# Expert loop of a mixture-of-experts kernel: gathers first, scatters two rounds behind them

## What is computed

```
scores = softmax(xf @ gate_w.T)                     # 2048 tokens, 64 experts
topk_w, topk_idx = top_k(scores, 6)
buf_tok, buf_w = per expert, its tokens and weights (capacity 128)
gx = xp[buf_tok]                                    # gather: [64, 128, 512]
g, u = split(gx @ gate_up_proj, 2)                  # per expert, 512 -> 2 x 192
eo = (silu(g) * u) @ down_proj * buf_w[..., None]   # per expert, 192 -> 512
routed = zeros.at[buf_tok].add(eo)                  # scatter-add
shared = (silu(xf @ sh_gate.T) * (xf @ sh_up.T)) @ sh_down.T
out = x + routed + shared
```

## Time and profile before

| | |
|---|---|
| median of 3 runs | 702.58 us (699.43 to 702.7) |
| the profiled execution | 701.51 us |
| its span, first to last instruction | 699.7 us |
| TensorE's mean granted clock | 0.92 |
| TensorE busy | 84% |
| GpSimd busy | 49% |
| GpSimd's queue: 27248 packets, 43.55 MB | 32.4% of the DMA engines' span |
| SyncE's queue: 48240 packets, 93.22 MB | 43.7% |

### The profile page before, as it was taken

How to read it: one execution, slowest core, us unless ns; L and a number is a source line. 1 busy time by engine, 2 the same in 40 slices (tenths; PEclk the granted TensorE clock), 3 DMA queues, 4 the chain that set the end, 5 groups by cost and what they waited for, 6 DMA issues and landing times. The chain is left out here.

```text
span 699.7 us, 6458 instructions
## 1 busy us (share of the span) xinstructions
PE 584.8 (84%) x2035; PEld 314.2 (45%) x2035; DVE 229.2 (33%) x575; ACT 172.9 (25%) x352; POOL 346.3 (49%) x299
## 2 busy tenths in 40 slices
PE   5998928776889999999998799997969999873950
PEld 2444414544534555555554455553535545441520
DVE  3865632865742322222222122221212222220220
ACT  4666742475101111112111111210101111110100
POOL 1134755262140656565642756556256565653662
PEclk9999959878989999999999899998989999897895
DMA  8945334569332989999889799988989999898752
GB/s 229 250 130 92 51 84 155 207 201 292 109 109 81 264 236 251 278 240 276 252 241 259 157 274 257 274 249 182 225 205 267 233 275 243 249 285 174 158 61 35
DMA packets 78170, 141.46 MB, mean 202 GB/s; under 512 B 14576, under 2 KB 33520, under 8 KB 78128
## 3 DMA queue, kind: packets, MB, share of 16 engines
q1 hardware_dynamic: 48240, 93.22, 43.7%
q0 software_dynamic: 27248, 43.55, 32.4%
q10 hardware_dynamic: 2640, 4.20, 1.7%
HBM read 107.89 MB, written 33.04 MB: 201 GB/s over the span
## 5 line engine op out<-in xcount | busy, mean ns | idle before, releaser
L507 POOL DMA_INDIRECT out<-y,half_at x128 | 200.6, 1567 | 191.6 <-DMA out<-y,half_at 59.2
L785 PE MATMUL bank<-gu_w,gxT 128*128 128x384 f32 x512 | 177.4, 490 | 0.8 <-ACT gxT L957 0.8
L773 PE MATMUL bank<-dn_w,hidT 96*128 96x512 f32 x256 | 125.4, 613 | 0.9 <-DVE hidT L1232 0.9
L1215 DVE TENSOR_SCALAR y<-bank,gx 128x512 f32<-128x512 f32 x64 | 48.0, 751 | 225.5 <-PE bank L773 202.4
L785 PEld LDWEIGHTS bank<-gu_w,gxT 128*128 128x128 f32 x512 | 93.2, 192 | 52.6 <-issue 2.5
L664 PE MATMUL bank<-xnT,upT 128*128 128x512 f32 x192 | 94.1, 636 | 0.0
L965 ACT ACTIVATE eg<-bank 128x192 f32<-128x192 f32 x64 | 21.1, 330 | 288.8 <-PE bank L785 288.8
L514 POOL DMA_INDIRECT gx<-rows_dram,table x64 | 64.3, 1005 | 21.7 <-issue 17.1
L1227 DVE TENSOR_TENSOR hid<-bank,eg 128x192 f32<-128x192 f32 x64 | 31.7, 496 | 130.7 <-ACT eg L965 130.7
L765 PE MATMUL bank<-ident,gx 128*128 128x128 f32 x256 | 41.3, 287 | 36.0 <-DMA gx<-rows_dram,table 35.8
L773 PEld LDWEIGHTS bank<-dn_w,hidT 96*128 96x128 f32 x256 | 47.5, 197 | 48.3 <-issue 46.8
(11 more groups left out here) (167 smaller groups left out, 465.1 us busy)
## 6 DMA issues: line engine op xcount, KB each, us to landing
gu_w<-in_gate_up SPq DMA_DIRECT2D x128, 384.0 KB, 4.6
dn_w<-in_down SPq DMA_DIRECT2D x128, 192.0 KB, 5.8
x<-in_x SPq DMA_DIRECT2D x4, 1024.0 KB, 9.0
feat_dram<-feat SPq DMA_DIRECT2D x16, 256.0 KB, 3.8
rows_dram<-rows ACTq DMA_DIRECT2D x4, 1024.0 KB, 4.8
out<-x SPq DMA_DIRECT2D x4, 1024.0 KB, 5.7
out<-x POOLq DMA_DIRECT2D x3, 1024.0 KB, 11.7
out<-y,half_at POOLq DMA_INDIRECT x128, 5.4
```

The lines of the kernel that those rows point to most:

```text
L507: pool.indirect_dma_start(halves, bass.IndirectOffsetOnAxis(ap=half_at[:, h, e:e + 1], axis=0), y[:, e % YB, h * (D // 2):(h + 1) * (D // ...
L773: last = nc.tensor.matmul(DN[:], hidT[:, e % 2, j, :], dn_w[:, e % U, j, :], start=(j == 0), stop=(j == 1))
L785: last = nc.tensor.matmul(GU[e % 2][:, 0:2 * I], gxT[:, e % 2, c, :], gu_w[:, e % U, c, :], start=(c == 0), stop=(c == KC - 1))
L1215: nc.vector.tensor_scalar(y[:, e % YB, :], DN[:], gx[:, e % GX, D + e:D + e + 1], None, ALU.mult).then_inc(y_ready, 1)
```

## The change

The loop runs over two more rounds. Each round asks first for the gather of expert e+6, then scatters both halves of expert e-2 and, where it is due, issues the shared add, which stands behind the same scatters as before. Nothing else is changed: buffers, waits and the programs of the other engines are the same.

```diff
+LAG = 2
...
-                for e in range(E):
-                    scatter(e, 0)
-                    scatter(e, 1)
+                for e in range(E + LAG):
                     if e + GX < E:
                         gather(e + GX)
-                    if e + 1 < E and shared_before(e + 1) > shared_before(e):
+                    if e < LAG:
+                        continue
+                    d = e - LAG
+                    scatter(d, 0)
+                    scatter(d, 1)
+                    if d + 1 < E and shared_before(d + 1) > shared_before(d):
                         for h in range(2):
-                            pool.wait_ge(half_added[h], 16 * (e + 1))
-                        add_shared(shared_before(e + 1))
+                            pool.wait_ge(half_added[h], 16 * (d + 1))
+                        add_shared(shared_before(d + 1))
```

## The result

The changed kernel takes 715.05 us, median of four runs (711.3 to 717.51); the kernel before took 701.93 us in its four (699.43 to 702.7). The ratio is 1.017, 95% interval 1.012 to 1.022: **slower by 13 us**. The forecast was 712.0 us. A second trace of the same kernel, taken with the experiments, has a span of 713.7 us and is set beside it where the two differ.

What follows compares the result with a forecast made beforehand. The prediction took the chain of half scatters, each waiting for the landing before, as the bound. Its terms, 14.0 + 3.9 - 2.2 - 5.2 = +10.5 us on 701.5, gave 712.0 us, range 699 to 721.

Steps and rivals of the forecast that it cites:

- chain of scatters: Half h of expert e starts only when half h of expert e-1 has landed; sets the end from expert 9 on.
- Start of the chain: At the loop's start, scatter 0 waits behind gather 8, which needs y(2): 240.5 instead of 226.5, +14.0 us.
- 369 to 373: Sign in the profile after: the time in us at which scatter 19 would start.
- low end of 10.6: If landings were quicker, y(21) would still hold scatter 19 to 369.1, so the late start costs at least +10.6 us.
- First shared add: Behind the first add, weights keep streaming, so rounds 22 and 23 lose their 5.05 us pace: +3.9 us, low end nothing.
- Second and third add: TensorE starved as before; half the difference between rounds of 23.8 and 19.4 us gained: -2.2 us, between 0 and -4.4.
- Tail: Last rounds: nine scatter rounds without gathers instead of six, four of them at 4.6 us: -5.2 us, or nothing.
- TensorE's waits: TensorE would wait for gathers less, 15 to 30 us, and none at the first add over 2 us.
- Rival A: Loop bound by feeding TensorE and the DMA engines; loaded scatter rounds fall to 6.6 us: -11, 690 us; chance 0.15.
- One sign that the forecast had named for A: Scatter rounds between the adds taking under 6.7 us would show the forecast wrong.
- Rivals B and C: B: no change, +1, 702.5 us, chance 0.11. C: weights stream through every add, +21, 723 us, chance 0.06.

Runs made afterwards that it cites:

- late lag: The kernel before up to scatter 19 and the first shared add, the order of the change from there on (gather e+8 ahead of scatter e): 698.2 us, ratio 1.000.
- no lag: The change with LAG 0 instead of 2, gather e+6 still ahead of scatter e: 711.6 us, ratio 1.019; measured again 708.3 us, 1.008.
- a lag of one: The change with LAG set to 1 instead of 2: 703.8 us, ratio to the kernel before 1.007.

## Why the prediction was right

It went through the chain of scatters instead of through TensorE's waits, and that was the step which decided. By its own steps:

- *Start of the chain*, +14.0: measured 14.9, of which 0.9 lies ahead of the loop. Scatter 0 stands at 241.37, forecast 240.5. At scatter 9 it is +16.9 (forecast 13.8), at scatter 19 +16.1 (forecast 14.0; the sign "369 to 373" became 374.63). The 2 us more at scatter 9 are a step that the forecast had wrong: it let scatters follow y there, at the 6.8 us a round of before, but scatter 9 starts 16.2 us behind its y, so from the first round on they waited for landings, at (304.54 - 241.37) / 9 = 7.0 us. The pace from 9 to 19 is 7.0 us, against 7.1 before: the chain gave back 0.8 us, where the low end of 10.6 had allowed 3.4.
- *First shared add*, +3.9 for lost fast rounds: measured +3.5 from scatter 20 to 23, by the mechanism named. The busy rows of 388 to 398 us before and of 393 to 414 us now (the last two numbers are DMA share and GB/s):

```profile
388.00:398.00 10.00, 9.56 (x22) 4.85 (x23) 1.08 (x2) 1.19 (x2) 8.17 (x7) 0.73 0.59 82
...
393.00:414.00 21.00, 20.82 (x69) 10.96 (x68) 5.40 (x11) 3.09 (x8) 12.47 (x9) 1.00 0.95 265
```

  Half scatters issued in these stretches landed in 3.8 us (median) before and in 6.5 now. What was missed is the add itself: from its issue to scatter 20 it took 10.5 us, 12.5 before, and the round was 3.4 us shorter (3.2 in the second trace). TensorE did not wait there: transposes 29 came at 405.4, forecast 404.5.
- *Second and third add*, -2.2: measured -0.9 and -0.9, inside the range of 0 to -4.4. In the second trace of the change the second add's round was 6.1 us shorter than before (17.7 us against 23.8), outside it. So this term isn't known to better than some 5 us.
- *Tail*, -5.2: measured -4.0 from scatter 54 to 58, then nothing. The pace of 4.6 us was right and the number of rounds was wrong: gather 63 stands behind scatter 54, so three rounds before scatter 58 became free, not four. Scatters 54, 55 and 58 are at 639.14, 644.26 and 662.71 before, and at 652.89, 658.68 and 672.53 now, so round 54 took 5.8 us (5.1 before) and rounds 55 to 57 took 4.6 each. Scatter 55 before and now, the second with gather 63 ahead of it:

```profile
644.26 1.58 POOL L507 DMA_INDIRECT out<-y,half_at  x1 [0.30 <-issue]
...
656.69 1.01 POOL L515 DMA_INDIRECT gx<-rows_dram,table  x1 [0.30 <-issue]
658.68 1.57 POOL L508 DMA_INDIRECT out<-y,half_at  x1 [0.98 <-DMA out<-y,half_at]
```

- Sum: +10.5 forecast, +9.9 in the trace, 13 between the medians. The range was 699 to 721. That the sum came within 1 us of the trace is partly luck: the shift ahead of the loop (+0.9), the rounds to scatter 9 (+2.0), the smaller gain of the second add and of the tail (+1.3 each) are cancelled by the first add's -3.4, the third's -0.9 and small terms between them. What the forecast had right is the path and its largest term, the late start.
- *TensorE's waits*, forecast 15 to 30 us: 34.2, so wrong. It waited 9.7 us behind the second add alone. The three rounds of lead were used up there, as forecast, and the same then happened in more, shorter waits. No price of it shows at the end of the chain; the last y came at 671.2, forecast 673.
- *Rival A* (feed TensorE and the DMA engines) would have had a landing under 5.5 us; it was 5.7 us in the same stretch, and 6.1 between the first two adds. One sign that the forecast had named for A did come: from scatter 37 to 53 a round took (634.38 - 527.83) / 16 = 6.66 us, under 6.7. It was a poor sign, for the kernel before has 6.72 there, and from scatter 20 to 36 a round took 7.0 us (6.7 before); neither stretch moved the way of A by more than 0.1. The page "Perfetto Trace Analysis" of the Trainium skill, in "Optimization Strategies", would have the engines optimized that block the critical path and leave the matmul engine idle. Here less idle time of TensorE was no gain as far as this chain lasts: a third less starvation by the late lag brought nothing, 46 us less matmul work brought 10. With half of the weight traffic gone TensorE itself was the bound, and there the rule would apply.
- *Rivals B and C* had the chain's rules right and took the ends of its terms; neither set of ends came.

## What to carry to other kernels

Before moving a request forward on an in-order queue, ask what the moved request itself waits for: whatever stands behind it now waits for that too. A software lag isn't free on a serial chain (here each scatter waits for the landing of the last): a late start of the chain is a late end, unless the chain has slack (5.6, 14.0 and 27.3 us later start made 5, 12 and 25 us here); begin the lag where the queue is behind already. And where an engine starves but its work finishes before the chain does, look for what interrupts the chain: taking three blocking adds out of it gained 12 us, and fed TensorE better than moving the gathers.

## What the hardware showed that I had not expected

The landing of a half scatter isn't a fixed latency with a small surcharge. It is 3.8 us with no weights beside it, 3.9 us with the DMA share at 0.76 and 169 GB/s, and 5.9 us with the share at 0.95 and 254 GB/s. Between them lies a stretch of the kernel with half of the weights, 381 to 470 us, without a shared add in it:

```profile
DMA to landing us min/median/max: 3.8/4.7/6.0
```

```profile
381.00:470.00 89.00, 89.00 (x296) 48.01 (x295) 22.75 (x43) 15.63 (x32) 61.90 (x46) 1.00 0.81 180
```

So up to three quarters of the load the landing hardly moves, and from there to nearly full it grows by half.

The landing of the 1 MB add differs between executions with no edit to the add: 11.5 to 14.1 us in the kernel before, 9.4 to 12.1 in the change, 9.1 to 10.1 in the second trace of the change. With no weights left, as the first of three at the end, it took 9.7. What makes the difference isn't shown.

The executions of one kernel spread more than the three shown at first, which lay within 0.5%: beside the experiments the kernel before ran from 692.8 to 711.2 us. Differences of 0.5% between kernels, as between no lag and a lag of one, can't be told apart by one comparison.
